# First routed unit's row maxima taken during the local rounds; last query chunks stored from the rope's tensors; unread products dropped

## The reference

```python
xn = _layernorm(x, axis=-1)
x = x + attn(xn, Wq, bq, Wk, bk, Wv, bv, Wo, bo, qn_w, kn_w, scale) + ffn(xn, W_gate, W_qkv)

def attn(x, ...):          # 16 query heads, 4 key/value heads, d_k = 32
    q, k, v = x @ Wq.T + bq, x @ Wk.T + bk, x @ Wv.T + bv
    q, k = rope(rmsnorm(q, qn_w)), rope(rmsnorm(k, kn_w))
    scores = einsum('bhqd,bhkd->bhqk', q, k) * scale       # causal, only the last 64 keys
    return softmax(masked scores) @ v, projected by Wo.T + bo

def ffn(x, W_gate, W_qkv): # "routed" attention
    gating = softmax(x @ W_gate.T); idx = argmax(gating)   # one of 16 heads per token
    q, k, v = split(x @ W_qkv.T, 3)
    k_shared, v_shared = k[head idx], v[head idx] * top gate value   # one key/value per token
    att = softmax(causal(q . k_shared / sqrt(32)))         # 16 heads, all earlier keys
    return att @ v_shared
```

## Time and profile before

| | us |
|---|---|
| three runs | 708.21, 709.88, 711.52 (median 709.88) |
| the profiled execution | 709.59 |
| its span, first to last instruction | 708.3 |
| mean granted TensorE clock | 0.978 |

### The profile page before, as it was taken

How to read it: one execution, slowest core, us unless ns; L and a number is a source line. 1 busy time by engine, 2 the same in 40 slices (tenths; PEclk the granted TensorE clock), 3 DMA queues, 4 the chain that set the end, 5 groups by cost and what they waited for, 6 DMA issues and landing times.

```text
span 708.3 us, 19515 instructions
## 1 busy us (share of the span) xinstructions
PE 658.4 (93%) x7450; PEld 517.0 (73%) x7450; DVE 499.0 (70%) x1345; ACT 363.9 (51%) x907; POOL 441.0 (62%) x366
## 2 busy tenths in 40 slices
PE   3788999999999999999977799799999999999997
PEld 3577778888788888787866467577777777777775
DVE  3967767657766675768645789688878787978544
ACT  4445435644355463364353056165656665656674
POOL 2875676934776737595922067276877777877740
PEclk9989999999999999999997899899999999999999
DMA  8513222231222321212236310310414040413011
GB/s 293 190 57 90 68 58 68 75 94 56 79 62 60 106 76 58 67 58 73 57 103 165 91 48 25 84 47 26 128 38 116 27 128 26 115 41 84 4 33 32
DMA packets 64014, 55.05 MB, mean 78 GB/s; under 512 B 6320, under 2 KB 48688, under 8 KB 63920
## 3 DMA queue, kind: packets, MB, share of 16 engines
q1 hardware_dynamic: 61760, 52.87, 25.4%
q10 hardware_dynamic: 2160, 0.93, 0.5%
HBM read 35.63 MB, written 17.89 MB: 76 GB/s over the span
## 4 chain that ended last, share of the span: by engine, by line
PE 74%; DVE 7%; POOL 5%; ACT 5%; DMA 4%; issue 3%; SPq 1%; ACTq 0%; DVEq 0%; POOLq 0%
PE gemm L901 15%; PE s_ps L1019 12%; PE od_ps L1075 10%; PE st_ps L1061 10%; PE gemm L987 5%; PE od_ps L1089 5%; PE gemm L897 3%; ACT p_loc L1463 3%; PE win L961 3%; PE win L946 2%; PE s_ps L1099 2%; DMA rope_t<-rope 2%; POOL rms_y L1572 2%; DVE l_sum L1246 2%; PE av L973 2%
## 5 line engine op out<-in xcount | busy, mean ns | idle before, releaser
L901 PE MATMUL gemm<-w_tok,xt 128*128 128x512 f32 (+1 forms) x768 | 184.5, 382 | 3.5 <-DVE qt L1229 1.4
L1296 DVE CUSTOM_DVE_ANT_0 s_ps<-s_ps,x_ln 128x512 f32<-128x512 f32 (+3 forms) x236 | 135.2, 624 | 29.5 <-PE s_ps L1019 28.9
L901 PEld LDWEIGHTS gemm<-w_tok,xt 128*128 128x128 f32 x768 | 129.8, 192 | 27.0 <-DVE qt L1229 1.8
L1019 PE MATMUL s_ps<-k_stack,w_tok 96*128 96x512 f32 (+2 forms) x360 | 113.1, 393 | 1.2 <-DVE picked_fk L1280 0.7
L1061 PE MATMUL st_ps<-w_tok,k_stack 98*128 98x512 f32 x288 | 101.3, 418 | 4.6 <-DMA w_tok<-w_tok 4.4
L1510 ACT ACTIVATE p_loc<-st_ps 128x512 f32<-128x512 f32 x144 | 77.1, 601 | 51.8 <-PE st_ps L1061 51.0
L1019 PEld LDWEIGHTS s_ps<-k_stack,w_tok 96*128 96x128 f32 x360 | 61.0, 192 | 32.9 <-DVE picked_fk L1296 14.8
L1296 DVE CUSTOM_DVE_ANT_0 s_ps<-s_ps,x_ln,picked_fk 128x256 f32<-128x256 f32 (+3 forms) x124 | 63.4, 561 | 9.1 <-PE s_ps L1019 8.9
L1463 ACT ACTIVATE p_loc<-win,l_max 128x96 f32<-128x96 f32 x256 | 61.1, 392 | 12.7 <-DVE l_max L1237 12.5
L1620 POOL TENSOR_TENSOR p_loc<-p_loc,l_rec 128x1536 f32<-128x1536 f32 x16 | 44.2, 2760 | 32.1 <-DVE l_rec L1249 32.0
L897 PE MATMUL gemm<-xt,w_qt 128*128 128x256 f32 x384 | 55.8, 293 | 8.1 <-DVE picked_fv L1191 4.4
(11 more groups left out here) (171 smaller groups left out, 1285.2 us busy)
## 6 DMA issues: line engine op xcount, KB each, us to landing
w_tok<-q_parts SPq DMA_DIRECT2D x96, 128.0 KB, 2.6
q_parts<-qt SPq DMA_DIRECT2D x128, 64.0 KB
x_ln<-x SPq DMA_DIRECT2D x8, 512.0 KB, 4.6
x_res<-x SPq DMA_DIRECT2D x16, 256.0 KB, 3.5
partial<-x_res SPq DMA_DIRECT2D x16, 256.0 KB, 2.0
k_t<-partial SPq DMA_DIRECT2D x8, 512.0 KB, 5.5
raw<-w_tok SPq DMA_DIRECT2D x3, 1024.0 KB, 13.7
v_win<-v_rows SPq DMA_DIRECT2D x64, 48.0 KB, 2.2
```

Of the source, the lines that this page charges most:

```text
L901: i = e.matmul(g[:, 0:cols], xs[l][:, k, a * P:(a + 1) * P], w_tok_p[r][:, k, c0:c0 + cols], start=first, stop=last)
L1019: e.matmul(s_ps[bank][:, 0:cols], q_op[b][0:HALVES, i, h, :], k_stack[0:HALVES, b * S + c0:b * S + c0 + cols], start=True, stop=True).then ...
L1296: e.tensor_tensor_reduce(out=s[:, 0:cols], in0=s[:, 0:cols], in1=causal[:, S - width + c0:S - width + c0 + cols], scale=1.0, scalar=dst if ...
```

## The change

- `first_maxima` becomes an ordinary chain of the rounds. For row block i it waits until round i // 2 has made its keys and stored query chunk 0, loads that block's queries into a new tensor `q_first` (step `first_q`, three DMAs, eight times), and takes the 4 or 8 pieces one by one in the bank `av`, which local values also use. Each piece waits in the planner until `av` is free, VectorE's backlog is below 2, and 4 (`MAX_EVERY`) have passed since the one before. Pieces without the diagonal are a plain `tensor_reduce`; the others add a small mask `diagonal`, made by GpSimd in round 0. The maxima lie in `r_first`, and are transposed in one go into one row.
- The stage after the joint has no maxima of unit 0.
- The last two query chunks of the last round go to `rope_b` and `rope_sq`, so their copies don't wait for earlier stores.
- The step `warm` is gone.
- `k_t` has one sequence's width; the residual of the routed stage is loaded into `w_tok1` and no longer into `k_t`.

```diff
+LAST_CHUNKS = [(ROUNDS - 1, 2), (ROUNDS - 1, 3)]
+MAX_EVERY = 4.0
...
 def take_qt(n, kind, c, freed):
+        if c == 0 and n < S // PAIR:
+            for _ in range(6):
+                yield None
+            p.q_kept = n
...
-            banks[:] = [0]
-            p.add(routed, 1, background=True)
...
+        while p.av_free is None or p.av_free > p.now:
+            yield None
+        p.av_free = None
+        p.take("av", ("values", m, a), ("at_lo", (m, a)))
         do("values", m, a)
...
     def first_maxima():
+        t, last = 0, 0.0
+        for i in range(IT):
+            while min(p.fk_stacked, p.q_kept) < i // 2:
+                yield None
+            do("first_q", i)
+            for _ in range(6):
+                yield None
+            while t < len(MAXIMA) and MAXIMA[t][0] == i:
+                while p.av_free is None or max(p.av_free, p.free["V"] - 2.0, last + MAX_EVERY) > p.now:
+                    yield None
+                p.av_free, last = None, p.now
+                p.take("av", ("first_max", t), ("first_max", t))
+                do("first_max", t)
+                cols = min((i + 1) * P - MAXIMA[t][2], 512)
+                def max_end(end):
+                    p.av_free = end + HOP
+                yield max(cols, 2 * P) * 0.00045, [("V", 0.1 + cols * 0.00105)], max_end
+                t += 1
+        while not p.rooms:
+            yield None
+        p.take("tp1", ("max_in_rows", 0), ("r_lo", 0))
+        do("max_in_rows", 0, 0)
...
-        self.maxima = [(0, t) for t in range(p.first_steps, len(MAXIMA) + 1)]
-        self.maxima += [(u, t) for u in range(1, UNITS_ROUTED) for t in range(len(MAXIMA) + 1)]
+        self.row_ready = {0: p.now}
+        self.maxima = [(u, t) for u in range(1, UNITS_ROUTED) for t in range(len(MAXIMA) + 1)]
...
-            if start - self.now >= WARM_FROM and u < UNITS_ROUTED and self.st_free[k % ST_BANKS] <= self.now:
-                self.do("warm", u, k, int((start - self.now - ROOM) / WARM))
...
             elif step == "first_max":                       # TensorE
+                t, = key
+                i, h, c0 = MAXIMA[t]
+                cols = max(min((i + 1) * P - c0, 512), 2 * P)
+                lane.wait_ge(*M["first_in"].of(i))
+                lane.wait_ge(*M["fk_out"].of(i // 2))
+                if free := freed("av", ("first_max", t)):
                     lane.wait_ge(*free)
+                e.matmul(first_scores[:, 0:cols], q_first[0:HALVES, h, :], k_stack[0:HALVES, c0:c0 + cols], start=True,
+                         stop=True).then_inc(*M["first_mm"].did(t))
...
             elif step == "first_max":                       # VectorE
+                lane.wait_ge(*M["first_mm"].of(t))
+                if c0 + cols < (i + 1) * P:
+                    e.tensor_reduce(dst, first_scores[:, 0:cols], AX.X, ALU.max).then_inc(*M["first_max"].did(t))
+                    continue
                 e.nop(nofuse=True)
                 e.tensor_tensor_reduce(
+                    out=first_scores[:, 0:cols], in0=first_scores[:, 0:cols], in1=diagonal[:, 512 - cols:512],
...
                 n, c = key                                  # ScalarE, qt
-                if n or c >= 2:
+                if (n, c) in LAST_CHUNKS:
+                    lane.wait_ge(*M["rope_sum"].of(last_tile))
+                    lane.wait_ge(*seq_squares(ROUNDS, 0))
+                elif n or c >= 2:
                     lane.wait_ge(*M[f"q_stored{c % 2}"].of((n, c - 2) if c >= 2 else (n - 1, c + 2)))
...
+            elif step == "first_q":                         # SyncE
+                i, = key
+                lane.wait_ge(*M["q_stored0"].of((i // 2, 0)))
+                if i:
+                    lane.wait_ge(*M["first_mm"].of([row for row, _, _ in MAXIMA].index(i) - 1))
+                for blk, part in ((0, 0), (1, 1), (2, 0)):
+                    e.dma_start(q_first[blk * DK:(blk + 1) * DK, :, :].bitcast(F32),
+                                q_parts[part, :, i, 0:HQ, :]).then_inc(*M["first_in"].did(i, inc=16))
```

More of the change, by code:

```diff
@@ L400, in first_maxima @@
     def first_maxima():
-        while p.fk_stacked < ROUNDS - 1 or bank_free[1] is None or bank_free[1] > p.now:
-            yield None
[L403 to L425, removed]
+        t, last = 0, 0.0
[13 more added lines that the diff above has]
+                def max_end(end):
+                    p.av_free = end + HOP
+                yield max(cols, 2 * P) * 0.00045, [("V", 0.1 + cols * 0.00105)], max_end
+                t += 1
+        while not p.rooms:
+            yield None
+        p.take("tp1", ("max_in_rows", 0), ("r_lo", 0))
+        do("max_in_rows", 0, 0)
+        yield 0.11, [("A", 0.27)]
+        do("max_low", 0, 0)
+        yield 0, [("V", 0.35)]
+        for _ in range(15):
+            yield None
     def when(product):
         return product[0]()
-    routed = first_maxima()
     do("x_load", 0)
@@ L434, in make_plan @@
     p.add(normalise(0), X_LANDS)
+    p.add(first_maxima())
     for n in range(ROUNDS):
         p.products.extend(product(n, unit) for unit in (UNITS if n < ROUNDS - 1 else LAST_UNITS))
-    p.run(when)
-    p.chains, p.alone = [], True
-    p.add(routed)
     p.run(when)
@@ L489, in take_low @@
     def take_low(self):
-        end, u, b, part, bank = self.later
+        end, u, b, bank = self.later
         self.later = None
-        self.do("max_low", u, b, part)
+        self.do("max_low", u, b)
         end = self.busy(max(end, self.now), ("V", 0.35))
         self.s_free[bank] = end + HOP
-        self.row_ready[u, part] = end + 2.6
+        self.row_ready[u] = end + 2.6
     def next_maximum(self):
@@ L515, in take_maximum @@
             self.s_free[bank] = None
-            self.later = (end, u, b, part, bank)
+            self.later = (end, u, b, bank)
             return
@@ L811, in mixed_attention_kernel, with max_rows, row_of @@
     p_sum = [Room(t).piece(HQ, P) for t in (cos_t, sin_t, *v_win[0], bias, bias_o)]
[L813 to L826, removed]
-        i0, count = (0, IT) if u else (part * PART, PART)
-        return q_op[b][HALVES + s:HALVES + s + 1, i0:i0 + count, :, :].bitcast(F32)
+    def max_rows(u):
+        return s_ps[plan.turn["s", ("max_in_rows", u)]][0:HQ * IT, 0:P] if u else tp1[0:HQ * IT, 0, :]
+    def row_of(b, s):
+        return q_op[b][HALVES + s:HALVES + s + 1, :, :, :].bitcast(F32)
     def turned_back(u, i):
@@ L837, in mixed_attention_kernel, with qt_of @@
     last_tile = (ROUNDS - 1, 1)
+    def qt_of(part, n, c):
+        if (n, c) in LAST_CHUNKS:
+            rooms = [t[:, :, :].rearrange("p h d -> p (h d)") for t in (rope_b, rope_sq)]
+            return rooms[c % 2][:, part * PAIR:(part + 1) * PAIR].bitcast(F32R)
+        return qt[part][:, c % 2, :]
     def raw_of(n):
```

164 lines of the change are left out of this document (76 added, 88 removed).

## The result

| | median us | runs | ratio to before | 95% interval |
|---|---|---|---|---|
| before | 710.15 | 14 | | |
| changed | 714.79 | 14 | 1.006 | 1.0041 to 1.0079 |

The forecast was 691.5 with a range of 680 to 705. The time is outside it, on the other side of no change. One run of before, 927.67, was disturbed and is left out of the ratio.

A forecast was written before the change was run, and what follows sets the result against it. It took the kernel as two saturated stages, TensorE the bound in the rounds, with a poor joint of some 100 us between. Rounds +16, joint -14, routed stage -20 give -18 against 709.59: 691.5 us, range 680 to 705.

The forecast's parts named there:

- TensorE's columns and VectorE's reductions in the rounds: Rounds: 48 products cost TensorE 8.9 us in full; VectorE's 26 us of maxima delay it 4; bank 1.5, hand-overs 1.
- Rival (a): Rounds: VectorE lags, so they grow by 28 to 32 us instead of 16; about 705 us; chance 0.13.
- rival (c): Rounds: maxima and values wait for the shared bank av, 0.6 us each, 38 us; total 725; chance 0.08.
- The loads of q_first: Rounds: eight query loads in SP's queue, 0.1 us of wait each, 1 us with what SP delays.
- Its upper bound, 8 us: Rounds: the most that waits for the query loads and SP's delays were taken to cost, from 0 to 8 us.
- The joint, -14: Between rounds and routed stage: joint ends at 386.8 instead of 400.8, 14 us sooner; bounds 5 and 17.
- Its 1.75, the reciprocal's 0.25 and the scaling's 2.75 with hops give 375.1: Joint: l_sum starts at 370 instead of 372.73; reduction, reciprocal and scaling follow, done at 375.1 instead of 377.59.
- the 4.02: Joint: the last query chunk's copy waits 4.02 us for a store ahead of l_sum; claimed to go.
- The routed stage, -20: Routed stage: unit 1's keys 38.9 us after its start instead of 57.3, gain 18.4; with clock 2, together 20; bounds 10, 25.
- The unread warming products ... give nothing when they go, except through the clock: Routed stage: these products stand in idle time, so removing them was given no gain except through the clock.
- The sign: Whole kernel: forecast 18 us faster; chance of faster 0.84, same 0.07, slower 0.09.
- wrong if the rounds grow by over 34 us: Rounds: the prediction's own limit for being wrong, growth over 34 us, beside a forecast of 16.

The follow-up runs named there:

- e1_other: Changed kernel, same order, but the 48 first-unit products take their stationary operand from the keys' tensor and never wait for a query load: 694.11 us, 0.9773.
- e8_chunks_undone: Changed kernel with the last two query chunks back in qt, waiting for the store of the chunk two before: 713.95 us, 1.0046.
- e10: Kernel before with one part of the change alone, the last two query chunks in the rope's tensors: 708.49 us, 0.998.
- e3_res: Changed kernel with the last round's residual loads and bias addition put ahead of the tile's attention: 710.82 us, 0.9998.
- e4_late: Changed kernel with 10 us planned, in place of six looks, between each round's first query request and its first product: 703.95 us, 0.9908.

## Why the prediction was wrong, step by step

- *TensorE's columns and VectorE's reductions in the rounds (8.9 + 4, with 1.5 and 1 for bank and hand-overs):* right in size, or a little high (the narrow products gave 5.3 us back for the columns' 8.9). From the first fk_stack transposes to the last qt product before takes 307.8 us (366.7 - 58.9), e1_other, which has all of this and no load waits, 319.7 (379.0 - 59.3): 11.9 us for 15.4 forecast. Rival (a), VectorE, and rival (c), the shared bank, are not what happened: narrowing VectorE gives 3.7 us back, and TensorE's waits on av for VectorE are 2.1 us in all. The +29.9 of the rounds lies in rival (a)'s +28 to +32, but by another mechanism.
- *The loads of q_first, "I take 0.1 us of wait each, 1 with what SP delays":* the step that failed. It is 11.4 us of waiting and up to 6.8 of clock, and e1_other gets back 17.6 in the rounds and 4 more in the joint. The sum of that step counted the load's own issue and landing (3.6 us) against 2.4 to 4.2 planned, and wrote down that SyncE is in order, but put the other transfers behind the load and not ahead of it: four stores of another chunk are 2.2 us, a window 1.8. The store of its own chunk, which it did count as a wait, held none of the loads that TensorE waited for. Its upper bound, 8 us, had no clock in it either, though the rows of the joint showed what idle time does to it.
- *The joint, -14:* the step "Its 1.75, the reciprocal's 0.25 and the scaling's 2.75 with hops give 375.1" failed. The scaling isn't next on GpSimd; the residual addition is. Before, its load stood behind four query stores and landed in 4.2 us (368.49 to 372.66); now it stands behind eleven issues and lands in 5.9 (402.16 to 408.02). The rope's rooms are not the reason, since in e8_chunks_undone, without them, the scaling starts at the same time. Before, that addition ended just ahead of the reciprocal and hardly showed; but it left 0.9 us of the 4.02 to gain, as e10 shows, and the step took the 4.02 as gone. e3_res takes the addition away: 22.6 us, against 20 forecast.
- *The routed stage, -20:* right: -20.8, and -20.8 in e1_other too. It rested on the steady period and on what unit 1 must wait for; unit 1's keys come 36.7 us after the stage's start for 38.9 forecast, and 57.3 before.
- *"The unread warming products ... give nothing when they go, except through the clock":* the exception was the thing, 2.7 us in the kernel before. In the changed kernel both stalls that they bridged are gone (clock 1.00 in every stretch of 5 us from 430 to 490), so it doesn't show in the 286.7.
- *The sign:* no rival had the load as its mechanism. The range ended at 705 because I let the gains of three parts stand as sure and gave the unmeasured queue the smallest share. Of 23.7 us of error, 13.9 are the rounds and 10.6 the joint, less 0.8 of the routed stage, and in both a load stands late in SyncE's queue; in the joint the order of GpSimd's work and a last projection at the half level, 2.4 us, come on top. The limit "wrong if the rounds grow by over 34 us" was too wide as well: they grew by 29.9.

## What to carry to other kernels

When work moves into a saturated stage and needs a transfer there, price the transfer from the queue: list what the issuing engine has ahead of it at that time, before its own issue and landing. In this kernel waits of 2.3 to 4.2 us for it were paid again in half-speed products. When a wait goes away, read what is next on each in-order engine of the chain, not only what is next in the data's chain; here an addition for another purpose was. And before a wait in a chain is counted as gained, look at what else ends just ahead of the same step: that it ended 0.9 us sooner was in the trace of the kernel before. When an edit changes a planner's order, read the starts of the stages and not the time alone: e4_late gained most of its time in another place than the one it was made for.

## What the runs showed of the hardware

- In this kernel waits of TensorE of 4.20, 3.13 and 2.32 us were followed by a granted clock of 0.78, 0.66 and 0.66 over a stretch of 5 us, a wait of 1.80 us by none below 1.00; the four waits cost 11.4 us directly and at most 6.8 by the clock.
- Seventeen unread products at two stalls kept the clock at 0.89 and 0.83 where it fell to 0.52 and 0.66 without them, worth 2.7 us.
- Taking 17.7 us of work from VectorE in rounds in which it was two thirds to three quarters busy gave back 3.7 us, with some 3.3 of doubt.
- 13 issues took SyncE 7 us (143.10 to 150.38 in e4_late), and the load behind them held TensorE for 4.88 us.
